# The opening of a fused two-layer block: context loads, norm statistics and the key transposes in another order

## The reference, cut to what matters

```python
x = x + tanh(g_xattn[0]) * L0_xattn(ctx, layernorm(x), Wq, Wk, gamma)   # ctx: (4, 256, 64), x: (4, 256, 256)
x = x + tanh(g_ffn[0])   * L0_ffn(layernorm(x), Wr, br, W1, W2)         # 16 blocks of 64, the best 4 are kept
x = x + tanh(g_xattn[1]) * L1_xattn(layernorm(x), ctx, ...)             # latent attention with rope
x = x + tanh(g_ffn[1])   * L1_ffn(layernorm(x), ...)                    # 32 experts, top 4

def L0_xattn(h, adj, Wq, Wk, gamma):
    sim  = heads(h @ Wq.T) . heads(h @ Wk.T) / 16          # 256 x 256 for each batch
    keep = sim >= (76th largest of each row of sim)
    A    = sigmoid(sim) * keep
    A    = (A + A.T) / 2
    return (1 - gamma) * adj + gamma * A                   # adj is layernorm(x)
```

## Time and profile before

| | us |
|---|---|
| median of 3 executions | 474.98 |
| lowest and highest | 474.36, 478.52 |
| the profiled execution's own time | 475.87 |
| its span (first to last instruction) | 474.0 |
| TensorE busy in the span | 438.7 (93%) |
| VectorE | 304.0 (64%) |
| ScalarE | 252.0 (53%) |
| GpSimd | 188.0 (40%) |

### The profile page before, as it was taken

One profiled execution on the slowest core, in us unless ns is written; L12 is line 12 of the kernel. 1 busy time (PEld: TensorE's weight loads), 2 busy tenths in 40 slices (PEclk: granted clock), 3 DMA queues, 4 the chain that ended last, 5 costly groups with the idle time before them and its releaser, 6 DMA issues. The chain is left out here.

```text
span 474.0 us, 8851 instructions
## 1 busy us (share of the span) xinstructions
PE 438.7 (93%) x2723; PEld 279.3 (59%) x2723; DVE 304.0 (64%) x886; ACT 252.0 (53%) x628; POOL 188.0 (40%) x190
## 2 busy tenths in 40 slices
PE   5886999899969999999999999999998899899987
PEld 2574877786734555555555555555566773644476
DVE  3989799955145766677676667757743748446612
ACT  3582445545314677667767766776666242045510
POOL 1650404041603566555465655546643005543000
PEclk9995999999977999999999999999999979999999
DMA  7643000000102343343334334212200799589202
GB/s 249 190 110 103 3 0 1 1 2 22 46 0 66 90 102 90 77 115 74 94 80 105 89 75 107 50 44 57 66 12 2 204 309 278 143 188 261 72 29 90
DMA packets 61448, 43.81 MB, mean 92 GB/s; under 512 B 22955, under 2 KB 54502, under 8 KB 61414
## 3 DMA queue, kind: packets, MB, share of 16 engines
q1 hardware_dynamic: 60646, 41.04, 32.6%
q0 software_dynamic: 768, 2.36, 2.5%
HBM read 27.25 MB, written 2.23 MB: 62 GB/s over the span
## 5 line engine op out<-in xcount | busy, mean ns | idle before, releaser
L1172 POOL TENSOR_TENSOR PB<-PB,inv 128x512 f32<-128x512 f32 x64 | 66.6, 1041 | 79.6 <-DVE inv L1222 79.4
L1111 ACT ACTIVATE PB<-ps,low 128x256 f32<-128x256 f32 x128 | 59.6, 471 | 31.0 <-DVE low L1216 31.0
L275 POOL TENSOR_TENSOR rot<-rot 128x512 f32<-128x512 f32 x48 | 61.1, 1273 | 32.6 <-DMA rot<-rot 32.6
L1216 DVE TENSOR_REDUCE low<-ps 128x2 f32<-128x512 f32 x64 | 44.1, 689 | 38.4 <-PE ps L1028 37.4
L255 DVE TENSOR_TENSOR rot<-ps,sinq 128x512 f32<-128x512 f32 x48 | 33.2, 692 | 16.6 <-PE ps L242 14.5
L1036 PE MATMUL ps<-ident,PB 128*128 128x128 f32 x256 | 41.1, 283 | 1.1 <-ACT PTS L1119 0.8
L1119 ACT ACTIVATE PTS<-ps 128x512 f32<-128x512 f32 x64 | 38.2, 597 | 7.2 <-PE ps L1036 5.1
L1036 PEld LDWEIGHTS ps<-ident,PB 128*128 128x128 f32 x256 | 27.7, 141 | 24.0 <-issue 19.9
L242 PE MATMUL ps<-XH,CH 128*128 128x512 f16 x96 | 37.6, 392 | 0.0
L242 PE MATMUL ps<-XL,CH 128*128 128x512 f16 x96 | 37.4, 390 | 0.0
L242 PE MATMUL ps<-XH,CL 128*128 128x512 f16 x96 | 37.4, 390 | 0.0
(11 more groups left out here) (246 smaller groups left out, 874.0 us busy)
## 6 DMA issues: line engine op xcount, KB each, us to landing
rot<-rot SPq DMA_DIRECT2D x64, 128.0 KB, 2.3
rot<-rot SPq DMA_DIRECT2D x64, 64.0 KB, 2.0
EGU<-in_L_ffn_W_gate_dram SPq DMA_DIRECT2D x8, 384.0 KB, 5.7
EGU<-in_L_ffn_W_up_dram SPq DMA_DIRECT2D x8, 384.0 KB, 5.8
ED<-in_L_ffn_W_down_dram SPq DMA_DIRECT2D x8, 384.0 KB, 6.6
rot<-in_L_ffn_W_dram SPq DMA_DIRECT2D x2, 1024.0 KB, 10.1
WQ<-in_L_xattn_Wq_dram SPq DMA_DIRECT2D x8, 256.0 KB, 3.0
WO<-in_L_xattn_Wo_dram SPq DMA_DIRECT2D x8, 256.0 KB, 3.1
```

The lines of the kernel that those rows point to most:

```text
L275: pool.tensor_tensor(g.RO[:, n, x, :], g.RO[:, n, x, :], g.TC[x][:, :], ALU.add).then_inc(g.sum_ok, 1)
L1111: e = act.activation(PB[t % 2][:, h, :], g.ps[:, SC + t % 2, h * S:(h + 1) * S], ACT.Exp, bias=low[:, t % 2, h:h + 1], scale=-1.0, accum_o ...
L1172: pool.tensor_tensor(PB[t % 2][:, :, :], PB[t % 2][:, :, :], inv[:, t % 2, :].unsqueeze(2).broadcast_to([P, 2, S]), ALU.mult).then_inc(nor ...
L1216: dve.tensor_reduce(low[:, t % 2, :], g.ps[:, SC + t % 2, :].rearrange("p (h s) -> p h s", h=2), AX.X, ALU.min).then_inc(low_ok, 1)
```

## The change

The context is loaded by ScalarE's queue, in two transfers: tiles 0 and 1 (batch 0, 64 KB) on `d_ctx`, the other six on `d_ctx2`. SyncE loads `wk`, `wq`, the first half of x, `ck`, `sk`, and then the second half of x, which now counts on `d_rope`. The context is turned and projected in three parts of 2, 2 and 4 tiles in place of two of 4. Batch 0's similarities are two fills, one for each tile, in banks of their own, each copied to `SIM` by itself, and both sigmoids follow the two copies. VectorE reads the statistics of x's first four tiles first, does rounds 0 to 2 of batch 0, and then the other four tiles and the rest of the statistics. `mixture()` stands behind round 8 instead of 7. The two fills of the keys come right behind the similarities (12 and 13), ahead of W1 (14 to 17), W2 (18 to 21), the router weights (22), the shared weights (23 to 25) and the folds (26 on); on ScalarE `KH` comes ahead of the tanh, the root and the copies of W1. `br` counts on `d_wr`. Left out of the diff below are that renaming and a few lines around it.

```diff
...
-def norm_stats(dve, g, nm, q):
+def norm_read(dve, g, nm, tiles):
+    for t in tiles:
+        dve.bn_stats(g.stat[:, t, :], g.X[:, t, :]).then_inc(nm.stats, 1)
+def norm_stats(dve, g, nm, q, done=0):
     n = nm.size
-    for t in range(n * q, n * q + n):
-        dve.bn_stats(g.stat[:, t, :], g.X[:, t, :]).then_inc(nm.stats, 1)
+    norm_read(dve, g, nm, range(n * q + done, n * q + n))
     for t in range(n * q, n * q + n):
...
-        N_CTX, N_G, N_V, N_SIM = (0, 4), 1, (2, 5), (3, 6, 7, 8)
-        N_W1, N_W2, N_WR, N_KV, N_SH, N_FOLD = 9, 13, 17, 18, 20, 23
-        is_split = [N_KV <= n < N_SH for n in range(N_FOLD + FOLDS)]
+        PARTS = ((0, 2), (2, 4), (4, 8))
+        N_CTX, N_G, N_V, N_FIRST, N_SIM = (0, 5, 7), 1, (2, 6, 8), 3, (4, 9, 10, 11)
+        N_KV, N_W1, N_W2, N_WR, N_SH, N_FOLD = 12, 14, 18, 22, 23, 26
+        is_split = [N_KV <= n < N_KV + 2 for n in range(N_FOLD + FOLDS)]
         splits = lambda n: sum(is_split[0:n + 1])
...
             def _(sp):
-                sp.dma_start(CT[:, :, :], c_v).then_inc(d_ctx, 16)
+                sp.dma_start(wk[:, :], i["L0_xattn_Wk"]).then_inc(d_wqk, 16)
                 sp.dma_start(wq[:, :], i["L0_xattn_Wq"]).then_inc(d_wqk, 16)
-                sp.dma_start(wk[:, :], i["L0_xattn_Wk"]).then_inc(d_wqk, 16)
-                for h in range(2):
-                    sp.dma_start(g.X[:, 4 * h:4 * h + 4, :], x_v[:, 4 * h:4 * h + 4, :]).then_inc(d_x, 16)
+                sp.dma_start(g.X[:, 0:4, :], x_v[:, 0:4, :]).then_inc(d_x, 16)
                 sp.dma_start(ck[:, :, :], i["cosk"]).then_inc(d_rope, 16)
                 sp.dma_start(sk[:, :, :], i["sink"]).then_inc(d_rope, 16)
+                sp.dma_start(g.X[:, 4:8, :], x_v[:, 4:8, :]).then_inc(d_rope, 16)
                 sp.dma_start(w1[:, :, :], i["L0_ffn_W1"].rearrange("(o p) n -> p o n", p=P)).then_inc(d_w1, 16)
...
                 pool.wait_ge(d_ctx, 16)
-                pool.wait_ge(d_rope, 32)
+                pool.wait_ge(d_ctx2, 16)
+                pool.wait_ge(d_rope, 48)
                 lt = lambda x: x.rearrange("p (b l) d -> p b l d", l=2)
...
                 pe.wait_ge(id_ok, 1)
+                def context(c):
+                    a, z = PARTS[c]
+                    o = bank(N_CTX[c])
+                    for t in range(a, z):
+                        mm = pe.transpose(o[0:DC, (t - a) * P:(t - a + 1) * P], CT[:, t, :], g.ident[:, :])
+                    mm.then_inc(filled, 1)
+                def projection(c):
+                    a, z = PARTS[c]
+                    o = bank(N_V[c])
+                    wait_empty(pe, max(N_G, N_CTX[c]))
+                    pe.matmul(o[0:DC, 0:(z - a) * P], GT[:, :], CTT[:, a * P:z * P],
+                              start=True, stop=True).then_inc(filled, 1)
+                def alike(o, b, j):
+                    return pe.matmul(o, CTT[:, (2 * b + j) * P:(2 * b + j + 1) * P], V[:, S * b:S * b + S],
+                                     start=True, stop=True)
+                def similarity(b):
+                    o = bank(N_SIM[b])
+                    wait_empty(pe, N_V[min(b, 2)])
+                    for j in range(2):
+                        mm = alike(o[:, S * j:S * j + S], b, j)
+                    mm.then_inc(filled, 1)
                 pe.wait_ge(d_ctx, 16)
-                def context(h):
-                    o = bank(N_CTX[h])
-                    for j in range(4):
-                        mm = pe.transpose(o[0:DC, j * P:(j + 1) * P], CT[:, 4 * h + j, :], g.ident[:, :])
-                    mm.then_inc(filled, 1)
-                def projection(h):
-                    o = bank(N_V[h])
-                    wait_empty(pe, max(N_G, N_CTX[h]))
-                    pe.matmul(o[0:DC, :], GT[:, :], CTT[:, 512 * h:512 * h + 512],
-                              start=True, stop=True).then_inc(filled, 1)
-                def similarity(b):
-                    o = bank(N_SIM[b])
-                    wait_empty(pe, N_V[b // 2])
-                    for j in range(2):
-                        mm = pe.matmul(o[:, S * j:S * j + S], CTT[:, (2 * b + j) * P:(2 * b + j + 1) * P],
-                                       V[:, S * b:S * b + S], start=True, stop=True)
-                    mm.then_inc(filled, 1)
                 context(0)
                 pe.wait_ge(d_wqk, 32)
                 pe.matmul(bank(N_G)[0:DC, 0:DC], wk[:, :], wq[:, :], start=True, stop=True).then_inc(filled, 1)
                 projection(0)
-                similarity(0)
-                context(1)
-                projection(1)
+                wait_empty(pe, N_V[0])
+                for j in range(2):
+                    alike(bank(N_FIRST + j)[:, 0:S], 0, j).then_inc(filled, 1)
+                pe.wait_ge(d_ctx2, 16)
+                for c in (1, 2):
+                    context(c)
+                    projection(c)
                 for b in range(1, B):
                     similarity(b)
+                pe.wait_ge(kv_ok, 1)
+                for h in range(2):
+                    o = bank(N_KV + h)
+                    for j in range(4):
+                        mm = pe.transpose(o[:, j * P:(j + 1) * P],
+                                          g.KV[:, 4 * h + j, :, :].rearrange("p a d -> p (a d)"), g.ident[:, :])
+                    mm.then_inc(filled, 1)
...
                     mm.then_inc(filled, 1)
-                pe.wait_ge(d_wr, 32)
+                pe.wait_ge(d_wr, 48)
                 o = bank(N_WR)
                 for k in range(KT):
                     pe.transpose(o[:, k * NBLK:(k + 1) * NBLK], wr[:, k * P:(k + 1) * P], g.ident[0:NBLK, 0:NBLK])
                 for k in range(KT):
                     mm = pe.transpose(o[:, S + k * E:S + (k + 1) * E], rw[:, k * P:(k + 1) * P], g.ident[0:E, 0:E])
                 mm.then_inc(filled, 1)
-                pe.wait_ge(kv_ok, 1)
-                for h in range(2):
-                    o = bank(N_KV + h)
-                    for j in range(4):
-                        mm = pe.transpose(o[:, j * P:(j + 1) * P],
-                                          g.KV[:, 4 * h + j, :, :].rearrange("p a d -> p (a d)"), g.ident[:, :])
-                    mm.then_inc(filled, 1)
...
                     return g.ps[:, n % 4, :]
-                def context(h):
-                    act.activation(CTT[:, 512 * h:512 * h + 512], bank(N_CTX[h])[0:DC, :],
+                act.dma_start(CT[:, 0:2, :], c_v[:, 0:2, :]).then_inc(d_ctx, 16)
+                act.dma_start(CT[:, 2:NT, :], c_v[:, 2:NT, :]).then_inc(d_ctx2, 16)
+                def context(c):
+                    a, z = PARTS[c]
+                    act.activation(CTT[:, a * P:z * P], bank(N_CTX[c])[0:DC, 0:(z - a) * P],
                                    ACT.Copy).then_inc(emptied, 1)
-                def projection(h):
-                    act.activation(V[:, 512 * h:512 * h + 512], bank(N_V[h])[0:DC, :], ACT.Copy,
+                def projection(c):
+                    a, z = PARTS[c]
+                    act.activation(V[:, a * P:z * P], bank(N_V[c])[0:DC, 0:(z - a) * P], ACT.Copy,
                                    scale=1.0 / 16.0).then_inc(emptied, 1)
...
                 projection(0)
-                similarity(0)
-                context(1)
-                projection(1)
+                for j in range(2):
+                    act.activation(SIM[:, j, :], bank(N_FIRST + j)[:, 0:S], ACT.Copy).then_inc(sim_ok, 1)
+                for j in range(2):
+                    act.activation(SIG[:, j, :], bank(N_FIRST + j)[:, 0:S], ACT.Sigmoid).then_inc(emptied, 1)
+                for c in (1, 2):
+                    context(c)
+                    projection(c)
                 for b in range(1, B):
                     similarity(b)
+                for h in range(2):
+                    act.activation(g.KH[:, 512 * h:512 * h + 512], bank(N_KV + h), ACT.Copy,
+                                   scale=-1.0).then_inc(hi_ok, 1)
                 act.wait_ge(d_raw, 80)
...
                 act.activation(g.rwT[:, :, :], o[:, S:S + KT * E], ACT.Copy).then_inc(emptied, 1)
-                for h in range(2):
-                    act.activation(g.KH[:, 512 * h:512 * h + 512], bank(N_KV + h), ACT.Copy,
-                                   scale=-1.0).then_inc(hi_ok, 1)
                 for n in range(3):
...
-                dve.wait_ge(d_x, 32)
-                norm_stats(dve, g, n0, 0)
+                dve.wait_ge(d_x, 16)
+                norm_read(dve, g, n0, range(NT // 2))
                 for b in range(B):
-                    dve.wait_ge(sim_ok, b + 1)
+                    dve.wait_ge(sim_ok, b + 2 if b else 1)
                     for r in range(ROUNDS):
                         for j in range(2):
                             if r > 0:
                                 dve.wait_ge(rep_ok, b * (ROUNDS - 1) * 2 + 2 * (r - 1) + j + 1)
+                            elif b == 0 and j == 1:
+                                dve.wait_ge(sim_ok, 2)
```

(35 more changed lines are left out.)

## The result

The changed kernel takes 479.56 us (median of 16 executions, 477.96 to 482.32) against 475.0 of the kernel before (16 executions, 473.95 to 478.52). The ratio is 1.009, 95% interval 1.007 to 1.011: 4.3 to 4.6 us slower, just inside one per cent.

The account below looks back on a forecast made before the run. VectorE and TensorE were taken to meet at `first(0)`, without slack behind. TensorE's weights, held by `KL`, make it 3.0 later and hide VectorE's 1.4 gain: 474.98 + 3.0 = 478.0 us, range 473.2 to 480.3.

Parts of the forecast that it names:

- The joint at `first(0)`: At 34.74 us VectorE and TensorE arrive together: an earlier VectorE alone gains nothing, a later TensorE costs in full.
- No slack behind it.: Behind `first(0)`, through batch 0's FFN and `symmetric(1)`: any shift of `first(0)` is carried to the end.
- Context first: Opening: 2.6 us less work for tile 0 and 0.4 from earlier landing; tiles in `SIM` at 7.9 and 8.8.
- Statistics in two parts: VectorE's opening: three rounds end at 12.8, the remaining statistics at 14.8; x's second half is covered by 1.6.
- The root: ScalarE, behind the keys' `KH`: done at 25.2 against 23.6 before, so `mixture()` waits 1.8 us.
- `KL` and the wait: `KL` at 26.8 holds back W1's third fill; TensorE goes on at 27.55 after idling from about 24.3.
- The clock: TensorE after the `KL` wait: 16 transposes at the lower level, then 20 at the higher; first fold +3.0 us.
- my third bullet: TensorE after the `KL` wait: all 36 transposes at the lower clock, first fold at 36.05, +5.2 us.
- Rival D: Clock stays low through transposes and folds: slower by over 1%, +9.1 us, 484; chance 0.08.
- B: Same wait for `KL`, but the weights' transposes run at the higher clock: 476.1; chance 0.20.
- C: Faster: new timing spares batch 0's FFN the slow stretch behind 38 us, up to 3.3 back: 473 to 475.5; chance 0.17.

Follow-up runs that it names:

- banks of its own: Changed kernel with the keys' two fills in banks 5 and 6, so no weight waits for `KL`: 474.52 against 474.71 us, ratio 0.9985.
- the kernel with 16 fillers: Changed kernel with 16 unread transposes of W1 into a free bank ahead of W1's third fill, wait for `KL` kept: 478.59 us, ratio 1.0074.

## Why the prediction was right, and where it was off

Forecast were 478.0 and a range of 473.2 to 480.3 with slower-within-one-per-cent as the likeliest; measured were 479.56. The mechanism, the wait for `KL` ahead of the weights at the lower clock, is the one that the runs show. Its size was forecast at 3.0 us and came out at 4.56.

- **The joint at `first(0)`.** Right. TensorE later by 4.61 at the first fold became 4.54 at `first(0)`. VectorE's gain lay inside the wait; it was 0.57 where 1.4 were forecast (29.66 against 28.8), and that cost nothing. The kernel with `symmetric(0)` ahead alone confirms the reading from the other side.
- **"No slack behind it."** Half right. The 4.54 grew to 5.45 at the next batch's `first`, as the slow stretch, 44.2 to 54.4 instead of 37.8 to 48.0, now covered more of batch 0's FFN, and the 5.45 were carried whole to 141 us. Then the stretches at the lower clock, which differ from one execution to the next, moved it to 3.6 in the two profiles, against 4.56 in the medians. That the medians come so near to the 4.54 at `first(0)` is in part luck.
- **Context first.** Forecast 7.9 and 8.8 for the two tiles in `SIM`, measured 7.78 + 0.38 = 8.2 and 9.0. The context landed at 2.98 rather than 3.3, but TensorE then waited 0.58 for `wq`. I had let the chain run through from the context's arrival and not costed that the second of the two small weights, issued at 1.38, lands only at about 4.1.
- **Statistics in two parts.** Right: 13.06 against 12.8, with no wait for x's second half.
- **The root.** Forecast 25.2, measured 25.62 + 0.21 = 25.8, because the last `SIM` copy stood at 21.62 and not at 20.8 to 21.0. I had taken the 12 similarity passes as unmoved, but the additional projection of tiles 2 and 3 and its copies stand ahead of them: the last projection started at 14.24, where I had 13.6.
- **`KL` and the wait.** The mechanism was right to the instruction, the times late by that 0.66: `KL` at 27.46 (26.8), W1's third fill at 28.19 (27.55). The experiment with banks of its own shows that the time goes with this wait, the fallen clock behind it included.
- **The clock: the term that was mis-sized.** I took 16 transposes at the lower level, +3.0 in all. The clock came back only at about 34.0, behind the 24 of W1 and W2 and most of the router's four, so the way from W1's third fill to the first fold took 7.23 and not 6.35. With the 0.66 that makes the first fold 1.5 us later than forecast. All of the weights at the lower level was my third bullet, +5.2; the truth lay between the two. The 16 was a count from one execution, and it is no constant: in the changed kernel the clock first rose behind the eight transposes of the keys and some two of W1 (the first eight of W1 took 1.27), in the kernel with 16 fillers only behind all 16 of both and some of the fillers.
- **Rivals.** The rule in the Trainium skill, TensorE: Matmul & The Clock Gate, Part 4 (PE-mode transpose), that transposes don't count for the clock, is contradicted again: in the changed kernel it rose at 34.0 behind nothing but transposes, and in the filled gap it rose among the 16 of them. Rival D put the median at 484; the highest of the 16 executions is 482.32. B (the clock stays up) failed at the gap: 0.50 behind it. A gain through the slow stretch behind 38 us (C) was not to be had: the stretch moved along, to 44.2.

## What to carry to other kernels

When a fill in a ring of banks moves, ask what its last reader is and when it comes: the fill n + 4 inherits that wait, and all fills behind it. Here the keys' last reader is VectorE in the midst of its rounds, and moving the fill ahead moved that reader's lateness ahead of 36 transposes. A wait that two engines reach at the same moment has to be bettered on both sides, and then on the next one behind it, before any of it shows. And two profiles compare only as far as their slow stretches are alike: the sum of a shift in the opening is best read ahead of the first stretch that differs between executions, here at 141 us, and beside the medians.

## What the runs showed of the hardware

The column of the granted clock reads 1.00 between 20.7 and 24.6 us of the changed kernel, though the eight transposes of the keys from 21.52 took 1.97, 0.22 each, as those at 0.50 did later. Early in a span the duration of like instructions tells the level, and the column doesn't.

How many transposes stood ahead of the rise differs: 16 in the kernel before, some 10 and, behind the standstill, 24 and part of the router's four in the changed kernel, over 20 in the one with 16 fillers.

At `first(0)` the standstill of 3.6 us cost more through the clock in the 5.9 us behind it (2.5) than by the wait itself (2.0); this is read from one profile each of three kernels. At the end of the kernel it could not be told apart so, since stretches near 140 us, at the lower clock for 3.6 to 10.4 us, moved the time by as much.
